# Attention exponentials turned by DMA instead of by TensorE, on eight cores

## The chip, the cores and the metric

The kernel runs on the 8 cores of one Trainium2 chip, each with a program of its own and no traffic between them. The time is the device time in microseconds (us) of the slowest core, the median of several runs. Core 2b+p takes batch row b and half of its query blocks (p is 0 or 1: even or odd blocks of 128), and for these everything that follows.

## What is computed

```
xn = layernorm(x)                                  # x: 4 x 2048 x 2048
q, k, v = split(xn @ w_atten.T)                    # 16 heads of 128
q, k = rope(q), rope(k)
att = softmax(causal(q @ k.T / sqrt(128)))
s = (att @ v) @ w_proj.T
h = silu(xn @ w_gate) * (xn @ w_up)                # 8192 wide
h = the 2 largest of each 4 by magnitude, others 0
out = x + s * silu(h @ w_down)
```

## The kernel before

Each of a core's five engine programs is written out by hand, with semaphores between them. The order is: layernorm of 16 tiles with their transposes and the first 15 units of the projections; the attention stage; 32 groups of the output projection; gate and up with the sparsification; down, and the end.

**Units and steps.** The q, k and v projections are cut into units (`UNITS`): one PSUM bank, 16 steps, a step being a matmul of 512 columns (L443) or two of 256 for v (L432). A group of two heads has 4 units of k and 2 of q for each head, and 8 of v. ScalarE copies a finished unit out of its bank (`leave`, L601 for q and k, L594 for v); for q and k two DMAs of 64 KB then swap the halves of the partitions (from SP, L352 and L353; for the first 15 units from ScalarE, L606 and L607) and VectorE applies rope in three instructions (L726, L728, L738), into one of three buffers of `qh` and `kh`. The weights come in pieces of 512 KB as POOL's DMAs into a ring of six (`ringA`), which the later stages extend to nine (`ringB`).

**Windows.** The attention stage has 128 windows, one for each head and each block of 128 queries; block j of a head has 256(j+1) keys. In window w TensorE computes the scores into PSUM banks 0 to 3 (L520; the mask is added by L522, a matmul with the identity), which needs the exponential of window w-1 to be done, as there is one set of these banks. VectorE takes the maximum (L807) and its negative (L811), ScalarE the exponential in f32 with its sum (L673), VectorE the reciprocal (L795) and the scaled block in bf16 (L801). TensorE fills the window with steps of the projections (`STEPS`, in two parts), and between the parts it transposes the scaled block of window w-1, 128 x 128 at a time, into bank 6 (first eight, L467) and bank 7 (the others, L474). VectorE copies the first eight out (L747), ScalarE the others (L615), into `pT`, which holds two blocks side by side. Every second window TensorE multiplies the values with both blocks (L491, v as weights, 256 columns moving), and ScalarE copies the result, already with d on the partitions, into `y_all` (L620).

Between the windows, SP's queue holds the rope swaps alone. The projection (L539) waits for the last copy to `y_all`.

## Time and profile before

| | us |
|---|---|
| median of 3 runs (2321.11 to 2322.1) | 2322.09 |
| the profiled execution's own time | 2320.11 |
| its span on the slowest core (of 2313.8 to 2318.6) | 2318.6 |
| TensorE busy | 2233.9 (96%) |
| VectorE busy | 996.6 (43%) |
| ScalarE busy | 635.7 (27%) |
| first scores of the attention stage, first projection matmul | 126.0, 903.3 |

The profile takes one execution. A busy time of TensorE counts each matmul from its start to a modelled end, so matmuls overlap; the chain of waits shows the distance between them. A wait is named by what released it. A line such as L467 is a line of the kernel before.

### The profile page before, as it was taken

To read this page: it belongs to the slowest core of one execution; us is meant where nothing else is said; L and a number is where in the kernel's file an instruction comes from. 1 tells how busy PE (TensorE), PEld (TensorE's weight loads), DVE (VectorE), ACT (ScalarE), POOL (GpSimd) and SP (SyncE) were. 2 spreads that over 40 slices of the span, in tenths; PEclk is the share of its full clock that TensorE was granted. 3 is DMA by queue.
4 is the path that set the end of the run, shared out by engine and by line. 5 is a ranking of instruction groups with operands and counts; after the bars stand their busy time and mean duration, and the time that the engine had idled before them with its cause. 6 is when DMAs were issued, how large, how long until landed. Compare 5 with 4: busy or idle time off the path is not lost.

```text
span 2318.6 us, 35747 instructions; the slowest of 8 cores (2313.8 to 2318.6 us)
## 1 busy us (share of the span) xinstructions
PE 2233.9 (96%) x12736; PEld 1181.9 (51%) x12736; DVE 996.6 (43%) x1441; ACT 635.7 (27%) x1082; POOL 137.5 (6%) x260
## 2 busy tenths in 40 slices
PE   4789999999999988999999999999999999999999
PEld 3547566675766744444444444444444444444444
DVE  5566867768677673004444443333333331000111
ACT  4624344444434434122222222222222200000000
POOL 0000000000000000000000000000000000000000
PEclk8999999999999999999999999999999999999999
DMA  9342322223122143754434344444554479766661
GB/s 268 109 79 47 61 40 45 57 44 66 38 46 56 33 79 74 156 111 80 83 74 73 73 80 83 90 94 91 97 101 94 91 168 238 157 127 132 132 138 44
DMA packets 82732, 217.38 MB, mean 94 GB/s; under 512 B 9984, under 2 KB 30592, under 8 KB 80000
## 3 DMA queue, kind: packets, MB, share of 16 engines
q0 software_dynamic: 36864, 134.23, 33.7%
q1 hardware_dynamic: 44576, 79.94, 11.0%
q8 instruction: 107, 1.75, 0.3%
q10 hardware_dynamic: 1120, 0.92, 0.1%
q14 instruction: 65, 0.53, 0.1%
HBM read 311.53 MB, written 25.17 MB: 145 GB/s over the span
## 4 chain that ended last, share of the span: by engine, by line
PE 82%; DVE 7%; issue 5%; DMA 3%; ACT 1%; DVEq 0%; ACTq 0%; SPq 0%
PE ps L554 37%; PE ps L573 19%; PE ps L432 8%; PE ps L443 7%; PE ps L539 5%; DVE arena L807 3%; DMA arena<-arena 2%; PE ps L520 2%; DVE arena L728 2%; PE ps L491 1%; PE ps L467 1%; DMA arena<-xN 1%; DVE arena L726 1%; PE ps L421 1%; DVE arena L738 1%
## 5 line engine op out<-in xcount | busy, mean ns | idle before, releaser
L554 PE MATMUL ps<-arena 128*128 128x512 bf16 x3968 | 856.6, 379 | 0.0
L554 PEld LDWEIGHTS ps<-arena 128*128 128x128 bf16 x3968 | 388.3, 98 | 468.1
L573 PE MATMUL ps<-arena 128*128 128x512 bf16 x2048 | 442.2, 379 | 1.1 <-DVE arena L858 1.1
L443 PE MATMUL ps<-arena 128*128 128x512 bf16 x1536 | 363.1, 385 | 14.2 <-ACT arena L630 14.2
L858 DVE TENSOR_TENSOR arena<-arena,ps 128x512 f32<-128x512 f32 x124 | 85.0, 685 | 633.7 <-PE ps L554 633.7
L573 PEld LDWEIGHTS ps<-arena 128*128 128x128 bf16 x2048 | 200.3, 98 | 242.9 <-issue 1.5
L432 PE MATMUL ps<-arena 128*128 128x256 bf16 x2048 | 241.1, 273 | 1.5 <-ACT arena L630 1.5
L443 PEld LDWEIGHTS ps<-arena 128*128 128x128 bf16 x1536 | 147.0, 99 | 167.6 <-issue 24.7
L696 ACT ACTIVATE arena<-arena 128x512 f32<-128x512 f32 x128 | 80.6, 630 | 519.5 <-DVE arena L858 519.5
L673 ACT ACTIVATE arena<-ps,arena 128x256 f32<-128x256 f32 (+7 forms) x128 | 156.4, 1222 | 230.9 <-DVE arena L811 230.8
L432 PEld LDWEIGHTS ps<-arena 128*128 128x128 bf16 x2048 | 197.1, 98 | 24.9 <-issue 1.8
L807 DVE TENSOR_REDUCE arena<-ps 128x1 f32<-128x256 f32 (+7 forms) x128 | 173.1, 1352 | 27.6 <-PE ps L522 26.7
L868 DVE TENSOR_TENSOR arena<-arena 128x512 f32<-128x512 f32 x32 | 22.2, 692 | 376.3 <-ACT arena L713 372.9
L713 ACT ACTIVATE arena<-ps 128x512 f32<-128x512 f32 x32 | 19.1, 597 | 422.7 <-PE ps L573 422.7
L898 POOL DMA_DIRECT2D arena<-wgu x128 | 67.5, 531 | 868.1 <-PE ps L554 710.8
L801 DVE TENSOR_SCALAR arena<-arena 128x256 bf16<-128x256 f32 (+7 forms) x128 | 104.9, 820 | 26.8 <-DVE arena L795 26.7
L539 PE MATMUL ps<-arena 128*128 128x512 bf16 x512 | 110.7, 379 | 0.6 <-ACT arena L620 0.6
L692 ACT ACTIVATE arena<-ps 128x512 f32<-128x512 f32 x124 | 73.8, 595 | 130.4 <-PE ps L554 130.4
L520 PE MATMUL ps<-arena 128*128 128x512 bf16 (+1 forms) x320 | 83.1, 358 | 18.8 <-ACT arena L673 14.2
L747 DVE COPY arena<-ps 128x1024 bf16<-128x1024 bf16 (+3 forms) x128 | 75.6, 591 | 51.0 <-PE ps L467 47.6
L728 DVE TENSOR_TENSOR arena<-arena 128x512 f32<-128x512 bf16 x96 | 65.9, 686 | 47.7 <-DMA arena<-arena 47.7
L539 PEld LDWEIGHTS ps<-arena 128*128 128x128 bf16 x512 | 50.0, 98 | 60.9 <-issue 0.8
(54 smaller groups left out, 1394.5 us busy)
## 6 DMA issues: line engine op xcount, KB each, us to landing
arena<-wgu POOLq DMA_DIRECT2D x128, 512.0 KB, 6.1
arena<-wd POOLq DMA_DIRECT2D x64, 512.0 KB, 5.8
arena<-wqkv POOLq DMA_DIRECT2D x48, 512.0 KB, 5.7
arena<-xN SPq DMA_DIRECT2D x16, 1024.0 KB, 12.7
arena<-arena SPq DMA_DIRECT2D x178, 64.0 KB, 2.1
arena<-wp POOLq DMA_DIRECT2D x16, 512.0 KB, 6.0
d_s<-arena SPq DMA_DIRECT2D x32, 256.0 KB, 4.0
d_hT<-arena SPq DMA_DIRECT2D x16, 512.0 KB, 6.7
```

Source lines behind the costliest of these rows:

```text
L432: mm = e.matmul(bank[:, (mi // NF) * 256:(mi // NF + 1) * 256], xnv[tc // 8][:, f, (tc % 8) * 128:(tc % 8 + 1) * 128], wv[f // 8][:, f % 8 ...
L443: mm = e.matmul(bank[:], w[:, f, :], xnv[tile // 2][:, f, (tile % 2) * 512:(tile % 2 + 1) * 512], start=(f == 0), stop=(f == NF - 1))
L520: mm = e.matmul(psum[:, c0:c1], qh[h % 3][:, j * 128:(j + 1) * 128], kh[h % 3][:, c0:c1], start=True, stop=(c1 != ncol))
L539: mm = e.matmul(ps[4 + k % 4][:], w[:, yc, :], yav[:, yc, half * 512:(half + 1) * 512], start=(yc == 0), stop=(yc == NF - 1))
L554: mm = e.matmul(ps[2 * p + up][:], w[:, f, :], xnv[0][:, f, half * 512:(half + 1) * 512], start=(f == 0), stop=(f == NF - 1))
L573: mm = e.matmul(ps[2 * (fc % 4) + half][:], w[:, j, :], hT[16 * q + j][:, half * 512:(half + 1) * 512], start=(q == 0 and j == 0), stop=(q ...
L673: e.activation(pexp[:, 0:ncol], psum[:, 0:ncol], AF.Exp, bias=nm[w % 2][:], scale=SCALE, accum_out=den[w % 2][:]).then_inc(S["a_ex"])
L696: e.activation(qv[half][:, r, :], h_sb[m % 2][:], AF.Square).then_inc(S["a_hq"])
L728: e.tensor_tensor(t2[:], xsw[r % 2][:], rsin[:, cols], ALU.mult).then_inc(S["v_t2"])
L801: e.tensor_scalar_mul(pbf[:, 0:ncol], pexp[:, 0:ncol], rc[b][:, 0:1]).then_inc(S["v_nr"])
L807: e.tensor_reduce(mx[b][:], psum[:, 0:ncol], mybir.AxisListType.X, ALU.max).then_inc(S["v_mx"])
L858: e.tensor_tensor(h_sb[m % 2][:], sg[m % 2][:], up[:], ALU.mult).then_inc(S["v_h"])
```

## The change

The exponential is written in bf16, without scaling, into one of two buffers `pexp`. SP turns it by one DMA transpose (`turn_p`, up to 128 x 2048) into one of four buffers `pT`. Three windows later (`LAG`) TensorE multiplies: now each 128 x 128 piece of `pT` is the weights and v moves, 128 columns, so that the result has the queries on the partitions. ScalarE copies it out times the reciprocal of the sum (`leave_y`), into `y_sb`, and SP turns it by a second DMA transpose into `y_all` (`turn_y`). The transposes on TensorE and both copies out of PSUM are gone, and so is VectorE's scaling. The rope swaps are issued from ScalarE throughout. The projections take a third PSUM bank. `STEPS` spreads the same number of steps in another way over the windows. The rings have five and eight buffers in place of six and nine.

```diff
-NRA, NRB = 6, 9
+NRA, NRB = 5, 8
+LAG = 3
...
-STEPS = [17, 18, 19, 20, 20, 21, 22, 23] * (2 * NG - 2)
-STEPS += [12, 13, 13, 14, 14, 14, 12, 12, 12, 12, 12, 13, 13, 13, 14, 15]
-def second_batches(w):
-    return 4 * ((w + 1) // NB) + max(0, (w + 1) % NB - 4)
+STEPS = [14, 15, 16, 21, 22, 23, 24, 25] * (2 * NG - 2)
+STEPS += [8, 9, 11, 16, 17, 19, 18, 18, 7, 8, 10, 12, 13, 13, 14, 15]
...
-    for w in range(NW + 1):
-        pv = (w - 3) // 2 if w % 2 == 1 and w >= 3 else None
-        if w < NW:
-            a = 7 if pv is not None else 9
-            parts = (cut(pos, pos + a), cut(pos + a, pos + STEPS[w]))
-            pos += STEPS[w]
-        else:
-            parts = ([], [])
-        rows.append((pv, parts))
+    for w in range(NW):
+        a = STEPS[w] // 2
+        rows.append((cut(pos, pos + a), cut(pos + a, pos + STEPS[w])))
+        pos += STEPS[w]
     assert pos == 16 * (len(UNITS) - NSTART)
-    return rows
+    return rows + LAG * [([], [])]
...
-    den = [A.alloc(1) for _ in range(2)]
-    rc = [A.alloc(1) for _ in range(2)]
+    den = [A.alloc(1) for _ in range(4)]
+    rc = [A.alloc(1) for _ in range(4)]
+    y_sb = [A.alloc(64, BF16) for _ in range(2)]
...
-    pexp = A.alloc(8 * KB)
-    pbf = A.alloc(4 * KB, BF16)
-    pT = A.alloc(8 * KB, BF16)
-    pTv = pT[:].rearrange("p (k x) -> p k x", x=256)
+    pexp = [A.alloc(4 * KB, BF16) for _ in range(2)]
+    pT = [A.alloc(4 * KB, BF16) for _ in range(4)]
+    pTv = [v[:].rearrange("p (k x) -> p k x", x=128) for v in pT]
...
-        def swap(r):
-            e.wait_ge(S["a_u"], ROPE_UNIT[r] + 1)
-            if r >= 2:
-                e.wait_ge(S["v_t2"], r - 1)
-            e.dma_start(out=xsw[r % 2][0:64, :], in_=raw[r % 2][64:128, :]).then_inc(S[f"dSW{r % 2}"], 16)
-            e.dma_start(out=xsw[r % 2][64:128, :], in_=raw[r % 2][0:64, :]).then_inc(S[f"dSW{r % 2}"], 16)
+        def turn_p(w):
+            e.wait_ge(S["a_ex"], w + 1)
+            if w >= 4:
+                e.wait_ge(S["p_pv"], w - 3)
+            n = 2 * (w % NB + 1)
+            e.dma_start_transpose(out=pTv[w % 4][:, 0:n, :], in_=pexp[w % 2][:, 0:128 * n]).then_inc(S[f"dT{w % 2}"], 16)
+        def turn_y(w):
+            h, j = w // NB, w % NB
+            e.wait_ge(S["a_y"], w + 1)
+            e.dma_start_transpose(out=yav[:, h:h + 1, j * 128:(j + 1) * 128], in_=y_sb[w % 2][:]).then_inc(S[f"dY{w % 2}"], 16)
...
+        for w in range(NW + LAG):
+            if w >= LAG:
+                turn_y(w - LAG)
+            if w < NW:
+                turn_p(w)
...
-                bank = ps[4 + u % 2]
-                if s0 == 0 and u >= 2:
-                    e.wait_ge(S["a_u"], u - 1)
+                bank = ps[4 + u % 3]
+                if s0 == 0 and u >= 3:
+                    e.wait_ge(S["a_u"], u - 2)
...
-        def turn_p(w):
-            n = 2 * (w % NB + 1)
-            e.wait_ge(S["v_nr"], w + 1)
+        def values(w):
+            h, n = w // NB, 2 * (w % NB + 1)
+            e.wait_ge(S[f"dT{w % 2}"], 16 * (w // 2 + 1))
+            e.wait_ge(S["a_u"], max(u for u, un in enumerate(UNITS) if un[:2] == (h // 2, "v")) + 1)
             if w:
-                e.wait_ge(S["v_te"], w)
-            for k in range(min(8, n)):
-                mm = e.transpose(psX[6][:, k, :], pbf[:, k * 128:(k + 1) * 128], id_sb[:])
-            mm.then_inc(S["p_t"])
-            if n > 8:
-                if second_batches(w - 1):
-                    e.wait_ge(S["a_te"], second_batches(w - 1))
-                e.wait_ge(S["a_y"], w // 2 if w % 2 == 0 else (w - 1) // 2)
-                for k in range(8, n):
-                    mm = e.transpose(psX[7][:, k - 8, :], pbf[:, k * 128:(k + 1) * 128], id_sb[:])
-                mm.then_inc(S["p_t1"])
-        def values(pair):
-            h, jj = pair // 4, pair % 4
-            e.wait_ge(S["v_te"], 2 * pair + 2)
-            if second_batches(2 * pair + 1):
-                e.wait_ge(S["a_te"], second_batches(2 * pair + 1))
-            if pair:
-                e.wait_ge(S["a_y"], pair)
-            bank = ps[7]
-            e.wait_ge(S["a_u"], max(u for u, un in enumerate(UNITS) if un[:2] == (h // 2, "v")) + 1)
+                e.wait_ge(S["a_y"], w)
             v = vg[(h // 2) % 2]
-            last = 4 * jj + 3
-            for k in range(last + 1):
-                x0 = 0 if k < 4 * jj + 2 else 128
-                mm = e.matmul(bank[:, x0:256], v[:, k * 256 + (h % 2) * 128:k * 256 + (h % 2 + 1) * 128],
-                              pTv[:, k, x0:256], start=(k == 0), stop=(k == last))
+            for k in range(n):
+                mm = e.matmul(ps[7][:, 0:128], pTv[w % 4][:, k, :],
+                              v[:, k * 256 + (h % 2) * 128:k * 256 + (h % 2 + 1) * 128],
+                              start=(k == 0), stop=(k == n - 1))
             mm.then_inc(S["p_pv"])
...
-            if pv is not None:
-                values(pv)
             steps(parts[0])
-            if w:
-                turn_p(w - 1)
+            if w >= LAG:
+                values(w - LAG)
             steps(parts[1])
-        values(NW // 2 - 1)
         for k in range(32):
...
-                e.wait_ge(S["a_y"], NW // 2)
+                e.wait_ge(S["a_u"], len(UNITS))
+                e.wait_ge(S["dY0"], 16 * (NW // 2))
+                e.wait_ge(S["dY1"], 16 * (NW // 2))
...
-                e.copy(raw[r % 2][:], ps[4 + u % 2][:]).then_inc(S["a_u"])
-                if u < NSTART:
-                    e.wait_ge(S["a_u"], u + 1)
-                    if r >= 2:
-                        e.wait_ge(S["v_t2"], r - 1)
-                    e.dma_start(out=xsw[r % 2][0:64, :], in_=raw[r % 2][64:128, :]).then_inc(S[f"dSW{r % 2}"], 16)
-                    e.dma_start(out=xsw[r % 2][64:128, :], in_=raw[r % 2][0:64, :]).then_inc(S[f"dSW{r % 2}"], 16)
-        def leave_p(w):
-            e.wait_ge(S["p_t1"], second_batches(w))
-            if w // 2:
-                e.wait_ge(S["p_pv"], w // 2)
-            n = 2 * (w % NB + 1) - 8
-            e.copy(pTv[:, 8:8 + n, (w % 2) * 128:(w % 2 + 1) * 128], psX[7][:, 0:n, :]).then_inc(S["a_te"])
-        def leave_y(pair):
-            h, jj = pair // 4, pair % 4
-            e.wait_ge(S["p_pv"], pair + 1)
-            e.copy(yav[:, h, jj * 256:(jj + 1) * 256],
-                   ps[7][:, 0:256]).then_inc(S["a_y"])
+                e.copy(raw[r % 2][:], ps[4 + u % 3][:]).then_inc(S["a_u"])
+                e.wait_ge(S["a_u"], u + 1)
+                if r >= 2:
+                    e.wait_ge(S["v_t2"], r - 1)
+                e.dma_start(out=xsw[r % 2][0:64, :], in_=raw[r % 2][64:128, :]).then_inc(S[f"dSW{r % 2}"], 16)
+                e.dma_start(out=xsw[r % 2][64:128, :], in_=raw[r % 2][0:64, :]).then_inc(S[f"dSW{r % 2}"], 16)
+        def leave_y(w):
+            e.wait_ge(S["p_pv"], w + 1)
+            e.wait_ge(S["v_rc"], w + 1)
+            if w >= 2:
+                e.wait_ge(S[f"dY{w % 2}"], 16 * (w // 2))
+            e.activation(y_sb[w % 2][:], ps[7][:, 0:128], AF.Copy, scale=rc[w % 4][:, 0:1]).then_inc(S["a_y"])
...
+        for w, parts in enumerate(WINDOWS):
             if w < NW:
                 ncol = 256 * (w % NB + 1)
                 e.wait_ge(S["v_nm"], w + 1)
-                if w:
-                    e.wait_ge(S["v_nr"], w)
                 if w >= 2:
-                    e.wait_ge(S["v_rc"], w - 1)
-                e.activation(pexp[:, 0:ncol], psum[:, 0:ncol], AF.Exp, bias=nm[w % 2][:], scale=SCALE,
-                             accum_out=den[w % 2][:]).then_inc(S["a_ex"])
-            if w and (w - 1) % NB >= 4:
-                leave_p(w - 1)
-            for u in LEAVE_LATE[w]:
+                    e.wait_ge(S[f"dT{w % 2}"], 16 * (w // 2))
+                if w >= 4:
+                    e.wait_ge(S["v_rc"], w - 3)
+                e.activation(pexp[w % 2][:, 0:ncol], psum[:, 0:ncol], AF.Exp, bias=nm[w % 2][:], scale=SCALE,
+                             accum_out=den[w % 4][:]).then_inc(S["a_ex"])
+            for u in ended(parts[0]):
                 leave(u)
-        leave_y(NW // 2 - 1)
+            if w >= LAG:
+                leave_y(w - LAG)
+            for u in ended(parts[1]):
+                leave(u)
...
-        def leave_p(w):
-            e.wait_ge(S["p_t"], w + 1)
-            if w // 2:
-                e.wait_ge(S["p_pv"], w // 2)
-            n = min(8, 2 * (w % NB + 1))
...
-        for w, (pv, parts) in enumerate(WINDOWS):
-            if w:
-                b, ncol = (w - 1) % 2, 256 * ((w - 1) % NB + 1)
-                e.wait_ge(S["a_ex"], w)
-                if w >= 3:
-                    e.wait_ge(S["v_nr"], w - 2)
-                e.reciprocal(rc[b][:], den[b][:]).then_inc(S["v_rc"])
-                e.wait_ge(S["v_rc"], w)
-                if w >= 2:
-                    e.wait_ge(S["p_t"], w - 1)
-                    if (w - 2) % NB >= 4:
-                        e.wait_ge(S["p_t1"], second_batches(w - 2))
-                e.tensor_scalar_mul(pbf[:, 0:ncol], pexp[:, 0:ncol], rc[b][:, 0:1]).then_inc(S["v_nr"])
+        for w in range(NW + 1):
...
-                    wait_piece_free(e, NA - NRA + b)
+                    wait_piece_free(e, NA - NRA + (b - NA) % NRA)
```

**TensorE, windows 7 and 8 of a head.** Before (L520 and L522 scores and mask, L443 and L432 steps, L467 and L474 transposes, L491 values of two blocks):

```order
L520 MATMUL ps<-arena 128x512 x3
L520 MATMUL ps<-arena 128x256
L522 MATMUL ps<-arena 128x256
L443 MATMUL ps<-arena 128x512 x9
L467 MATMUL ps<-arena 128x128 x8
L474 MATMUL ps<-arena 128x128 x4
L443 MATMUL ps<-arena 128x512 x13
L520 MATMUL ps<-arena 128x512 x4
L522 MATMUL ps<-arena 128x256
L491 MATMUL ps<-arena 128x256 x10
L491 MATMUL ps<-arena 128x128 x2
```

After (L496 and L498 scores and mask, L429 steps, L466 values of one block):

```order
L496 MATMUL ps<-arena 128x512 x3
L496 MATMUL ps<-arena 128x256
L498 MATMUL ps<-arena 128x256
L429 MATMUL ps<-arena 128x256 x24
L466 MATMUL ps<-arena 128x128 x8
L429 MATMUL ps<-arena 128x256 x24
```

The 12 transposes between the steps are gone; in their place stand the 8 value matmuls of the block three windows before, and the window has 24 steps (48 matmuls of 256 columns), where it had 22 (of 512 there).

**ScalarE, from the exponential of a head's seventh block to the eighth's or past it.** Before (L673 exponential, L615 copy of transposes, L601 exit of a q or k unit, L620 exit of y):

```order
L673 ACTIVATE arena<-ps,arena 128x1792
L615 COPY arena<-ps 128x4x128
L601 CAST arena<-ps 128x512
L620 CAST arena<-ps 128x256
L601 CAST arena<-ps 128x512
L673 ACTIVATE arena<-ps,arena 128x2048
L615 COPY arena<-ps 128x6x128
L601 CAST arena<-ps 128x512
L673 ACTIVATE arena<-ps,arena 128x256
```

After (L637 exponential, L576 exit of a unit, L580 and L581 its swap, L589 exit of y with the scaling):

```order
L637 ACTIVATE arena<-ps,arena 128x1792
L576 CAST arena<-ps 128x512
L580 DMA arena<-arena 64x512
L581 DMA arena<-arena 64x512
L589 ACTIVATE arena<-ps,arena 128x128
L576 CAST arena<-ps 128x512
L580 DMA arena<-arena 64x512
L581 DMA arena<-arena 64x512
L637 ACTIVATE arena<-ps,arena 128x2048
L576 CAST arena<-ps 128x512
L580 DMA arena<-arena 64x512
L581 DMA arena<-arena 64x512
```

The copy of transposes is gone, and behind every exit of a q or k unit stand two DMA issues ahead of the next instruction.

**SP, the attention stage.** Before (L352, L353 swaps), with the waits:

```order
L353 DMA arena<-arena 64x512
L352 DMA arena<-arena 64x512 [waits a_u,v_t2]
L353 DMA arena<-arena 64x512
L352 DMA arena<-arena 64x512 [waits a_u,v_t2]
L353 DMA arena<-arena 64x512
L352 DMA arena<-arena 64x512 [waits a_u,v_t2]
```

After (L343 the exponentials' transposes, L349 y's):

```order
L343 DMA_TRANSPOSE arena<-arena 128x16x128 [waits a_ex,p_pv]
L349 DMA_TRANSPOSE arena<-arena 128x1x128 [waits a_y]
L343 DMA_TRANSPOSE arena<-arena 128x2x128 [waits a_ex,p_pv]
L349 DMA_TRANSPOSE arena<-arena 128x1x128 [waits a_y]
L343 DMA_TRANSPOSE arena<-arena 128x4x128 [waits a_ex,p_pv]
L349 DMA_TRANSPOSE arena<-arena 128x1x128 [waits a_y]
```

The swaps have left the queue; a transpose of y that waits for ScalarE's exit stands ahead of each transpose of exponentials.

## Rows read from the trace of the kernel before

**Rows 1.** The table of stretches (busy time and instructions of each engine, granted clock, DMA share, GB/s)

```profile
126.00:898.00 772.00, 744.89 (x5568) 486.30 (x5568) 553.72 (x910) 312.62 (x535) 28.38 (x51) 1.00 0.27 52
260.00:700.00 440.00, 431.81 (x3315) 291.03 (x3314) 318.97 (x524) 179.08 (x306) 13.72 (x26) 1.00 0.25 48
800.00:898.00 98.00, 85.72 (x611) 49.97 (x609) 67.18 (x109) 42.56 (x71) 7.27 (x11) 1.00 0.35 63
```

**Rows 2.** TensorE's waits, 126 to 915 us (total, times, longest)

```profile
PE ps L520 <- ACT arena L673: 14.2, 23, 2.2
PE ps L467 <- DVE arena L801: 11.0, 17, 2.1
```

**Rows 3.** The chain of waits, 500 to 530 us (start, us, what)

```profile
507.36 0.45 PE ps L467 x8
...
508.03 2.84 PE ps L432 x26
...
515.35 3.45 PE ps L443 x16
...
523.91 1.64 PE ps L491 x16
```

**Rows 4.** Groups by form, whole span (busy, mean ns, idle before)

```profile
L491 PE MATMUL ps<-arena 128*128 128x256 bf16 x512 | 67.7, 276 | 2.6 <-ACT arena L615 2.6
...
L467 PE MATMUL ps<-arena 128*128 128x128 bf16 x832 | 67.2, 219 | 11.7 <-DVE arena L801 11.0 <-issue 0.5
...
L474 PE MATMUL ps<-arena 128*128 128x128 bf16 x320 | 28.3, 219 | 0.0
...
L491 PE MATMUL ps<-arena 128*128 128x128 bf16 x128 | 17.6, 219 | 0.0
```

**Rows 5.** The page, costliest groups: VectorE's scaling and copies

```profile
L801 DVE TENSOR_SCALAR arena<-arena 128x256 bf16<-128x256 f32 (+7 forms) x128 | 104.9, 820 | 26.8 <-DVE arena L795 26.7
...
L747 DVE COPY arena<-ps 128x1024 bf16<-128x1024 bf16 (+3 forms) x128 | 75.6, 591 | 51.0 <-PE ps L467 47.6
```

**Rows 6.** TensorE's waits, 800 to 898 us

```profile
PE ps L467 <- DVE arena L801: 2.1, 1, 2.1
```

**Rows 7.** The chain of waits, 885 to 915 us

```profile
890.01 2.30 DVE arena L807
...
894.69 0.20 ACT arena L673
...
899.57 3.13 PE ps L491 x16
...
903.30 11.81 PE ps L539 x54
```

**Rows 8.** Groups by form, VectorE's maximum and ScalarE's exponential of a first block

```profile
L673 ACT ACTIVATE arena<-ps,arena 128x256 f32<-128x256 f32 x16 | 7.6, 474 | 27.7 <-DVE arena L811 27.7
...
L807 DVE TENSOR_REDUCE arena<-ps 128x1 f32<-128x256 f32 x16 | 6.7, 421 | 0.6
```

**Rows 9.** The page, DMA issues (count, KB each, us to landing)

```profile
arena<-wqkv POOLq DMA_DIRECT2D x48, 512.0 KB, 5.7
...
arena<-arena SPq DMA_DIRECT2D x178, 64.0 KB, 2.1
...
d_hT<-arena SPq DMA_DIRECT2D x16, 512.0 KB, 6.7
```

**Rows 10.** Instructions in order of time, TensorE, 126 to 136 us

```profile
126.03 0.37 PE L520 MATMUL ps<-arena 128*128 128x256 bf16 x1 [4.55 <-DVE arena L738]
...
126.41 6.05 PE L443 MATMUL ps<-arena 128*128 128x512 bf16 x17
```

**Rows 11.** Instructions in order of time, ScalarE, 95 to 126 us

```profile
122.40 0.47 ACTq L606 DMA_DIRECT2D arena<-arena  x1
122.90 0.71 ACTq L607 DMA_DIRECT2D arena<-arena  x1
```

**Rows 12.** VectorE's waits, 126 to 915 us

```profile
DVE arena L728 <- DMA arena<-arena: 31.2, 23, 4.5
```

35 lines of the change are left out of this document (14 added, 21 removed).

## The prediction

> **What bounds the kernel now.** I read the table of stretches first, then TensorE's waits, the chain of waits, and last the single forms and the DMA issues. The stretch that the change touches is the attention stage, from the first scores at 126 us [rows 10] to the first projection matmul at 903.3 [rows 7], so 777 us. The table shows TensorE busy for 744.9 us of its first 772, at a granted clock of 1.00 (2.4 GHz), VectorE for 554 and ScalarE for 313; in the 440 us from 260 to 700 TensorE idles 8.2 us in all [rows 1]. TensorE's waits of the whole stage are short: 14.2 us on the exponential before the next scores, 11.0 on the scaled block before its transposes [rows 2]. So TensorE's own work is the bound, and a matmul taken away there comes off the time, as long as what replaces it keeps up.
>
> The chain of waits gives the spacing of back to back matmuls, which the busy times (219 or 272 ns each) hide: 8 transposes in 0.45 us, so 0.056 us each; 26 matmuls of 256 columns in 2.84, so 0.109; 16 of 512 columns in 3.45, so 0.2155; 16 of the values in 1.64, which is 14 x 0.109 + 2 x 0.056 [rows 3]. The last one matters: a value matmul of 128 columns, with its own weight load, also costs 0.056.
>
> **The change part by part.** Where no sign of time is given, it is TensorE's path in the attention stage.
>
> 1. The transposes go. There are 832 + 320 of them [rows 4]; 1152 x 0.056 = **-64.5 us**.
>
> 2. The values are turned round and done per block of 128 queries. Before: 512 x 0.109 + 128 x 0.056 = 63.0 us [rows 3, 4]. After: 72 matmuls per head of 128 columns, 1152 x 0.056 = 64.5. **+1.5 us**.
>
> 3. VectorE loses the scaling of the exponentials (104.9 us) and the copies out of PSUM (75.6) [rows 5], ScalarE the second copies. That is no time by itself, but TensorE's waits for the scaling go with it; of their 11.0 us, 2.1 lie between 800 and 898 us [rows 6] and are counted next, the other 8.9 here: **-9 us**. Between 800 and 898 us TensorE idles 12.3 us [rows 1], because the last windows hold few projection steps and the chain scores, maximum, exponential is longer than TensorE's work. That chain stays, without the scaling in VectorE's way. For the last block of a head it is 0.97 of scores and mask, 0.15 to start, and from 890.01 to 894.89 maximum and exponential [rows 7]: 6.1 us; for the first 2.0 (maximum 0.42, exponential 0.47 [rows 8]), and the six between them spaced evenly. Against it stands TensorE's work by the new step counts. In the last head, 15 steps x 0.2155 + 0.97 + 10 values x 0.056 = 4.8 for the last block; over its eight windows the chain exceeds the work by 4.6 us, over those of the head before by 1.0. So 12.3 becomes 5.6: **-7 us**. In all other heads the work of a window (3.9 us with 14 steps, 6.9 with 25) is above its chain (2.0 to 6.1), so nothing is added there.
>
> 4. The tail. Before, from the end of the last exponential at 894.89 to the projection at 903.30 it is 8.4 us: scaling, 16 transposes, copies, 16 value matmuls in 3.13 us (half the clock), copy [rows 7]. Now: issue 0.5, landing of 512 KB, 16 values at the low clock 1.8, their exit 0.4, issue 0.5, landing of y 2.1, 0.2 of semaphores. The landing of a 512 KB transpose is in no row; plain transfers of that size took 5.7 and 6.7 us, 64 KB within SBUF 2.1 [rows 9]; I take 6.2. Sum 11.7, so +3.3. Steps 1 and 2 counted 1.6 us of this stretch as saved, which goes back on. The projection starts cold: after the 4.55 us pause that ended at 126 us, 17 matmuls took 6.05 in place of 3.66 [rows 10], +2.4. Together **+7 us**.
>
> 5. The transposes of all other blocks are hidden if two limits hold. Latency: an exponential waits for the transpose of two blocks before, since there are two buffers. It is tightest behind the last block of a head, followed by the two shortest windows: 0.8 us left of its own window, 3.9 of the next and 1.6 of the second until ScalarE wants the buffer, so 6.3, and 1.8 more (4.3 of work less 2.5 of chain) until TensorE waits for the scores' bank. The values come three windows later, 14 us or more. A landing of 6.2 just fits. Throughput: a head needs 72 + 8 blocks of 32 KB in 43.3 us of TensorE's work (160 steps, 3.9 us of scores, 0.9 of masks, 4.0 of values), so up to 0.54 us a block costs nothing. Rows give 5.7 to 6.7 us for 16 blocks' bytes, 0.36 to 0.42 a block, at their whole latency; at the other end the swaps of rope, 64 KB in 2.1, give 1.05 [rows 9]. I take the nearer in size, the 512 KB ones: **0 us**, and keep 1.05 for a rival.
>
> The Trainium skill, VectorE: DVE Perf Modes, The three transpose paths, speaks against this: it gives 1309 ns for a 128 x 128 transpose by DMA against 390 on TensorE. One after the other, the DMA ones would make 80 x 1.309 = 105 us a head and, as an estimate, 3220 us for the kernel. Its 390 ns is a lone instruction: the trace has 56 ns in a row [rows 3], so the 1309 is likely to be latency as well. The Trainium skill's DMA: Bandwidth & Descriptors, Latency and other measured facts, has 261 GB/s for DMA transposes, by which 512 KB move in 2.0 us; an estimate by that page leaves the sum as it is. No run here shows either.
>
> 6. The swaps of rope move from SP's queue to ScalarE's. SP's queue is then the transposes' alone: it issues the y of three blocks before, then the block's own; y waits for the middle of the window, which is before the exponential's end for the long blocks and 1 us after it for the shortest. On ScalarE two issues take 0.47 and 0.71 [rows 11], so 82 units put 97 us on an engine that is busy for 313 of 772 [rows 1], and each issue stands ahead of an exponential or an exit. A window has 0.8 to 1.9 us of slack against its chain. Where two rope units end in one window (2 x 1.9 us with their exits, exponential 2.2, y 0.4) ScalarE is just inside 6.9. VectorE waited 31 us for swaps in this stage already [rows 12], and transposes now share the rings. Between nothing and 0.4 us for each of 82 (33 us) I take **+6 us**, near the low end, as VectorE has 180 us less to do.
>
> 7. The ring of five and eight, one bank more for the projections: POOL waits long for free pieces today, a piece lands in 5.7 us [rows 9], and eight units (some 36 us) lie between the release that decides and the use. 0. If the ring were late, TensorE would wait at a first step of a unit; I see no place.
>
> Sum: -64.5 + 1.5 - 9 - 7 + 7 + 6 = **-66 us** on the profiled execution's 2320.1 us (span 2318.6 and 1.5 around it), so 2254. The median of the runs is 2.0 above that execution: **2256 us**.
>
> **Rivals.** A measurement of this kernel can tell about 0.2% (4.6 us) from no change.
>
> A. As summed, 56%. Its own range is 2244 (no cost in step 6, and a landing of 4 us) to 2280 (step 6 at 0.4 us each).
>
> B. Faster, but a wait takes back about half. ScalarE's queue, with swap issues that also wait for rope's second product two units before, delays exponentials, and swaps land behind 512 KB transposes, so that VectorE holds the next maximum. At 0.4 us for each unit plus the DVE wait of 31 us doubled and half exposed: 2256 + 27 + 15 = 2298. For it: one swap in four already makes VectorE wait. Against: a swap has most of a window. 16%.
>
> C. The other side. The transposes are slower than TensorE: SP's single queue turns one block at a time, and the bound is 80 blocks a head. At the swap's 1.05 us a block a head takes 84 us, the stage 1344, the kernel 2322 + 567 = 2889. It binds from 0.54 us a block, and loses from 48.6 / 80 = 0.61; at 0.67 it is 2400. For it: small rows within SBUF are the only such transfers the trace has, and their rate is low. Against: large ones run at 0.4. 24%, a third of it below 2400; 5 of the 24 for blocks that go one at a time at over 1.05 us each, towards the 2.1 us of a whole swap, which would be over 2889. The Trainium skill's 1309 ns (The three transpose paths) would lie there, at 3220 by the estimate above.
>
> D. No change. If each value matmul waited for its weight load, they would be spaced 0.109 instead of 0.056: 1152 x 0.053 = +61 us, 2317 or, with the rest of step 6, 2322. The 16 value matmuls in 1.64 us [rows 3] speak against it. 4%.
>
> **The numbers.** Faster by over 0.2%: A and B, 0.72. Same: D, 0.04. Slower: C, 0.24. Range 2244 to 2400: below it 2% of A, above it about 16% of C.
>
> **What would show it.** Right: no transposes on TensorE in the attention stage, 1152 value matmuls in 0.056 us each by the chain, stage of 711 us at the full clock, transposes of 512 KB landing in under 8 us, ScalarE's exponential waiting for the maximum and not for a DMA, a pause of 10 us before the projection. Step 5 is wrong if the exponentials wait for DMA or SP's queue is never idle; step 6 if TensorE's scores wait for an exponential that came behind a swap. A stage over 777 us makes the prediction wrong in sign.

## The result: slower by 1.4%, where 2.8% faster was forecast

The change takes 2352.10 us (2351.69 to 2361.73), the kernel before 2322.1 (2321.11 to 2323.11). The ratio is 1.0142, with a 95% interval of 1.0112 to 1.0173. In some executions of either kernel the cores of one or both dies show a lower clock and the time is some per cent longer; these are left out of every time and ratio here (with the one of 2679.2 us the median of the change is 2356.91, the 2357 of the expectations below). The forecast was 2256 us: the time lies in its range of 2244 to 2400, on the wrong side. In the profile of the change cores 0 and 1 show a granted clock of 0.81 for some 115 us; the stage is therefore compared on core 5 below, which has none of it and whose span is nearly as long.

The spans of the changed kernel by core, with the mean granted clock (before: 2313.8 to 2318.6, 0.992 to 0.994):

```profile
core 1: 2360.0 us, clock 0.965
...
core 4: 2331.8 us, clock 0.979
core 5: 2357.5 us, clock 0.978
```

The whole attention stage in the table of stretches, core 5. First the kernel before:

```profile
126.00:903.30 777.30, 748.07 (x5585) 488.44 (x5586) 554.19 (x910) 314.13 (x538) 28.38 (x51) 0.99 0.27 52
```

the change:

```profile
123.00:940.70 817.70, 711.80 (x4944) 446.01 (x4945) 393.37 (x655) 284.29 (x539) 26.92 (x51) 0.94 0.62 101
```

This is where the time is. The stage was to shrink from 777 to 711 us and grew to 817.7. TensorE has its matmuls taken away (busy 748 to 712), yet idles 105.9 us where it idled 29.2. The granted clock falls from 0.99 to 0.94: it was at half (1.2 GHz) for 92 us of this stage on core 5, for 67 to 92 on the eight cores, before for 8 to 17. VectorE has lost 161 us of its work (554.19 to 393.37). The DMA engines' share went from 0.27 to 0.62.

What ended the waits in the stage, core 1 (engine, line, releaser; total, times, longest). The scores are L496 now, the exponential L637, the value matmuls L466, rope's product with the swap L693:

```profile
DVE arena L693 <- DMA arena<-arena: 103.7, 33, 8.3
PEld ps L496 <- issue: 99.7, 63, 8.0
PE ps L496 <- ACT arena L637: 79.7, 29, 7.6
...
ACT arena L637 <- DMA arena<-arena: 53.4, 10, 10.6
...
PE ps L466 <- DMA arena<-arena: 4.6, 1, 4.6
```

Against [rows 2]: TensorE's wait for the exponential before the next scores rose from 14.2 us to 79.7. The waits for the scaling are gone, and TensorE hardly waits for the turned block itself. The late ones are one step earlier: ScalarE waits for a DMA, 10 times and up to 10.6 us, which is the transpose (here called a turn) of two windows before, and VectorE waits for rope's swaps (31.2 us in [rows 12]).

The page of the change, groups and DMA issues (the value matmuls, then the issues with us to landing last):

```profile
L466 PE MATMUL ps<-arena 128*128 128x128 bf16 x1152 | 93.2, 231 | 8.7 <-DMA arena<-arena 4.6
...
arena<-wqkv POOLq DMA_DIRECT2D x48, 512.0 KB, 6.5
arena<-arena ACTq DMA_DIRECT2D x192, 64.0 KB, 2.8
```

The pieces landed in 5.7 us before, the swaps in 2.1 [rows 9].

**One such wait from the start.** Core 1, 482 to 500 us, in order of time (start, us; in brackets the idle time before and its releaser). The exponential of a head's seventh block ends at 479.37, and y's exit (L589) of three blocks before stands on ScalarE behind an exit and two swap issues:

```profile
479.18 0.19 ACT L637 ACTIVATION_READ_ACCUMULATOR arena<-ps,arena 128x1 f32 x1
...
481.30 0.37 ACT L589 ACTIVATE arena<-ps,arena 128x128 bf16<-128x128 f32 x1 [1.45 <-issue]
```

SP's queue, where L349 is the turn of y and L343 that of a block (the one at 482.99 the seventh block's, the one at 489.67 the eighth's):

```profile
481.74 1.10 SPq L349 DMA_TRANSPOSE arena<-arena  x1
482.99 1.44 SPq L343 DMA_TRANSPOSE arena<-arena  x1
488.42 1.11 SPq L349 DMA_TRANSPOSE arena<-arena  x1
489.67 8.02 SPq L343 DMA_TRANSPOSE arena<-arena  x1
```

POOL's queue, which loads the weight pieces:

```profile
483.34 0.53 POOL L833 DMA_DIRECT2D arena<-wqkv  x1 [17.53 <-PE ps L440]
```

ScalarE, with the swaps that it issues:

```profile
486.52 0.47 ACTq L580 DMA_DIRECT2D arena<-arena  x1
487.02 0.74 ACTq L581 DMA_DIRECT2D arena<-arena  x1
...
497.65 0.47 ACT L637 ACTIVATE arena<-ps,arena 128x256 bf16<-128x256 f32 x1 [8.84 <-DMA arena<-arena]
```

VectorE, then TensorE:

```profile
489.04 0.69 DVE L691 TENSOR_TENSOR arena<-arena 128x512 f32<-128x512 bf16 x1
497.90 0.69 DVE L693 TENSOR_TENSOR arena<-arena 128x512 f32<-128x512 bf16 x1 [8.17 <-DMA arena<-arena]
```

```profile
489.15 1.67 PE L440 MATMUL ps<-arena 128*128 128x512 bf16 x7
498.36 0.59 PE L496 MATMUL ps<-arena 128*128 128x512 bf16 x1 [7.54 <-ACT arena L637]
```

The chain of waits over the same stretch has the transfer itself as one piece:

```profile
482.99 14.52 DMA arena<-arena
```

The turn of the seventh block (1792 columns, 448 KB) leaves at 482.99, 3.6 us after its exponential, as y's turn stands ahead of it and waits for the exit. A 512 KB weight piece follows 0.35 us later. The turn lands at 497.51, after 14.5 us, where I had 6.2 for a larger one. SP's next turn of a block takes 8 us to issue. The two swaps issued at 486.52 and 487.02, 64 KB each, land at 497.42 and 497.81, so two things are late at once: ScalarE may not write the buffer that is being turned, and VectorE stands in rope with the next maximum behind it. TensorE has used up its steps and stops for 7.5 us, and then goes on at half the clock:

```profile
484.00:489.00 5.00, 5.00 (x33) 2.49 (x31) 4.42 (x9) 3.23 (x5) 0.00 (x0) 1.00 1.17 103
498.40:501.00 2.60, 2.60 (x10) 1.41 (x11) 2.22 (x5) 0.08 (x1) 0.45 (x1) 0.50 0.53 118
```

From the trace's DMA records, over all cores, and counting a weight piece as in flight when over 20 of its packets move during the turn: the turn of a head's seventh block (448 KB) lands in 4.0 us (median) without one and in 9.1 with one (longest 4.8 and 15.4), that of the eighth in 5.9 and 8.8. Of 128 turns a core, 26 to 30 take over the 6.3 us that step 5 allowed; 212 of these 226 have a piece in flight. A turn also leaves late: on the eight cores 1.6 to 3.6 us after the end of its exponential (medians by block of a head; 3.2 for the seventh, 2.6 for the eighth), behind y's.

### The profile page after: what moved, and what is told of

Its sections match the earlier page's. It is cut to its first block, busy times and chain, and to the rows that moved or that the text cites. A ratio compares the mean times of both kernels' runs of the same rounds, so it can differ in the third digit from the quotient of the medians.

```text
span 2360.0 us, 34216 instructions; the slowest of 8 cores (2331.8 to 2360.0 us)
## 1 busy us (share of the span) xinstructions
PE 2218.7 (94%) x12096; PEld 1148.6 (49%) x12096; DVE 835.4 (35%) x1185; ACT 604.6 (26%) x1082; POOL 135.8 (6%) x260
## 4 chain that ended last, share of the span: by engine, by line
PE 81%; DMA 10%; DVE 3%; issue 3%; ACT 2%; ACTq 1%; SPq 0%; DVEq 0%
PE ps L529 36%; PE ps L548 19%; PE ps L429 9%; DMA arena<-arena 9%; PE ps L440 7%; PE ps L514 5%; PE ps L496 2%; PE ps L466 2%; DVE arena L752 1%; DMA arena<-xN 1%; DVE arena L693 1%; ACT arena L576 1%; ACTq L580 1%; DVE arena L722 0%; ACT arena L637 0%
## 5 line engine op out<-in xcount | busy, mean ns | idle before, releaser
L529 PE MATMUL ps<-arena 128*128 128x512 bf16 x3968 | 856.6, 379 | 0.0
L529 PEld LDWEIGHTS ps<-arena 128*128 128x128 bf16 x3968 | 388.3, 98 | 468.2
L548 PE MATMUL ps<-arena 128*128 128x512 bf16 x2048 | 442.2, 379 | 1.1 <-DVE arena L808 1.1
L440 PE MATMUL ps<-arena 128*128 128x512 bf16 x1536 | 385.5, 400 | 13.1 <-ACT arena L598 13.1
L548 PEld LDWEIGHTS ps<-arena 128*128 128x128 bf16 x2048 | 200.3, 98 | 242.9 <-issue 1.5
L637 ACT ACTIVATE arena<-ps,arena 128x256 bf16<-128x256 f32 (+7 forms) x128 | 156.3, 1221 | 432.7 <-DVE arena L762 347.4
L429 PE MATMUL ps<-arena 128*128 128x256 bf16 x2048 | 252.5, 281 | 1.0 <-ACT arena L598 1.0
L440 PEld LDWEIGHTS ps<-arena 128*128 128x128 bf16 x1536 | 153.3, 102 | 181.1 <-issue 63.3
L429 PEld LDWEIGHTS ps<-arena 128*128 128x128 bf16 x2048 | 204.5, 101 | 34.2 <-issue 4.2
L496 PE MATMUL ps<-arena 128*128 128x512 bf16 (+1 forms) x320 | 87.7, 374 | 82.0 <-ACT arena L637 79.7
L514 PE MATMUL ps<-arena 128*128 128x512 bf16 x512 | 112.9, 384 | 3.0 <-DMA arena<-arena 3.0
L693 DVE TENSOR_TENSOR arena<-arena 128x512 f32<-128x512 bf16 x96 | 66.0, 687 | 120.5 <-DMA arena<-arena 120.5
L466 PE MATMUL ps<-arena 128*128 128x128 bf16 x1152 | 93.2, 231 | 8.7 <-DMA arena<-arena 4.6
L466 PEld LDWEIGHTS ps<-arena 128*128 128x128 bf16 x1152 | 82.3, 105 | 34.8 <-issue 19.2
L496 PEld LDWEIGHTS ps<-arena 128*128 128x128 bf16 x320 | 30.2, 99 | 121.3 <-issue 102.5
## 6 DMA issues: line engine op xcount, KB each, us to landing
arena<-xN SPq DMA_DIRECT2D x16, 1024.0 KB, 10.8
```

The source lines that it names most:

```text
L429: mm = e.matmul(bank[:, (mi // NF) * 256:(mi // NF + 1) * 256], xnv[tc // 8][:, f, (tc % 8) * 128:(tc % 8 + 1) * 128], wv[f // 8][:, f % 8 ...
L440: mm = e.matmul(bank[:], w[:, f, :], xnv[tile // 2][:, f, (tile % 2) * 512:(tile % 2 + 1) * 512], start=(f == 0), stop=(f == NF - 1))
L466: mm = e.matmul(ps[7][:, 0:128], pTv[w % 4][:, k, :], v[:, k * 256 + (h % 2) * 128:k * 256 + (h % 2 + 1) * 128], start=(k == 0), stop=(k = ...
L496: mm = e.matmul(psum[:, c0:c1], qh[h % 3][:, j * 128:(j + 1) * 128], kh[h % 3][:, c0:c1], start=True, stop=(c1 != ncol))
L514: mm = e.matmul(ps[4 + k % 4][:], w[:, yc, :], yav[:, yc, half * 512:(half + 1) * 512], start=(yc == 0), stop=(yc == NF - 1))
L529: mm = e.matmul(ps[2 * p + up][:], w[:, f, :], xnv[0][:, f, half * 512:(half + 1) * 512], start=(f == 0), stop=(f == NF - 1))
```

## The experiments

All ratios are against the kernel before, run on the same chip between them (2323.3 us for the first four, 2325.6 for e5 to e8, 2324.9 for e9 to e12, 2324.4 for the last two), and compare means, so that a time quoted below, a median, can differ from them a little. The table below gives, from each trace, the range over the eight cores. "Maxima late" is how much later than the usual 0.12 us after the end of the scores the maximum began, summed over 128 blocks; "exponentials late" is the same from the negative maximum to the exponential. Not all of either stops TensorE, as the first row shows: the kernel before has its maxima later still, but in short pieces. TensorE waited over 2 us before a block's scores 2 or 3 times in its stage, 15 to 19 times in the change's and once or twice in e13's.

| kernel | ratio, 95% | stage, us | TensorE idle | half clock | maxima late | exponentials late |
|---|---|---|---|---|---|---|
| before | | 775–779 | 26–36 | 8–17 | 115–126 | 17–18 |
| the change | 1.0142 (1.0112 to 1.0173) | 788–818 | 87–106 | 67–92 | 93–107 | 45–76 |
| e1 small swaps | 1.0014 (0.9983 to 1.0045) | 766–782 | 74–86 | 37–64 | 86–99 | 41–55 |
| e2 small pieces | 0.9844 (0.9760 to 0.9928) | 729–753 | 44–53 | 21–33 | 54–59 | 40–48 |
| e3 both | 0.9838 (0.9786 to 0.9891) | 721–733 | 37–51 | 14–33 | 49–53 | 41–50 |
| e4 plain copies | 0.9963 (0.9929 to 0.9997) | 753–774 | 65–77 | 22–60 | 99–112 | 26–33 |
| e5 three buffers | 1.0154 (1.0087 to 1.0221) | 776–809 | 73–98 | 62–91 | 107–130 | 27–37 |
| e6 late rope | two runs: 0.997, 1.002 | 763–773 | 67–89 | 46–63 | 13–17 | 106–126 |
| e7 quarters | 1.0042 (1.0018 to 1.0067) | 765–774 | 71–87 | 36–58 | 73–88 | 65–76 |
| e8 all three | 0.9833 (0.9817 to 0.9850) | 723–733 | 39–52 | 27–38 | 14–21 | 47–57 |
| e9 whole start | 0.9776 (0.9731 to 0.9822) | 716–740 | 35–55 | 23–45 | 11–22 | 48–62 |
| e10 late, quarters | 1.0027 (1.0016 to 1.0037) | 749–779 | 59–84 | 34–52 | 13–16 | 109–142 |
| e11 late, three | 0.9855 (0.9806 to 0.9903) | 726–743 | 42–55 | 28–43 | 17–27 | 50–66 |
| e12 before, swaps moved | 1.0017 (1.0005 to 1.0029) | 776–788 | 30–43 | 6–14 | 110–123 | 27–32 |
| e13 last burst spread | 0.9716 (0.9692 to 0.9739) | 708–721 | 27–43 | 18–25 | 11–20 | 42–49 |
| e14 three, quarters | 0.9893 (0.9862 to 0.9925) | 732–749 | 44–59 | 22–43 | 74–86 | 27–32 |

**Less to move: e1 to e4.** These four move other data than the kernel needs, and so compute something else. The change with swaps of 16 columns in place of 512 after the first 15 units:

```diff
+                m = 512 if u < NSTART else 16
-  ...xsw[r % 2][0:64, :], in_=raw[r % 2][64:128, :]...
+  ...xsw[r % 2][0:64, 0:m], in_=raw[r % 2][64:128, 0:m]...
```

> The change, with the rope swaps of the attention windows cut to 16 of 512 columns (same DMAs, waits and order; q and k are wrong). Theory S (the swaps land late behind the transposes, and VectorE, which runs its work in order, holds the next maximum for them): VectorE's waits for DMA in the windows (74 us between 260 and 800 us) fall only if the bytes matter; if the swap's packets stand behind those of a transpose, a small swap lands as late and the time stays at 2352 to 2360. Theory P (ScalarE's issues of the swaps are what costs): unchanged, 2357. Theory B (it is the bytes of the swaps): about 45 us of TensorE's waits go, and half of the cold clock behind them, 2300.

2325.05 us, 1.3% under the change: between theory B's 2300 and the unchanged time of the others. But VectorE's wait for the swaps hardly moved in the profile, from 120.5 us over the span to

```profile
DVE arena L694 <- DMA arena<-arena: 109.3, 36, 9.3
```

though a swap carries 1/32 of the bytes. So a swap is late mostly through what is ahead of it or beside it, not through its own size; what fell a little are the long turns (20 to 25 of 128 over 6.3 us) and the half clock. The weight pieces cut to 64 of 2048 columns from the seventh on:

```diff
+                m = 2048 if n < 6 else 64
-                e.dma_start(out=ringA[p % NRA][:], in_=wqkv[p])...
+                e.dma_start(out=ringA[p % NRA][:, 0:m], in_=wqkv[p][:, 0:m])...
```

> The change, with the weight pieces of the attention stage from the seventh on cut to 64 of 2048 columns (same DMAs, waits and order; the projections are wrong). Theory C (collision: a transpose and a weight piece in flight together slow each other, turns of the seventh block land in 7 to 15 us in place of 4.4): the turns land in 4 to 6 us, ScalarE's exponential no longer waits for DMA, about 30 us of TensorE's waits and the cold clock behind them go: 2300 to 2315. Rival T (the transposes alone are slow enough, since two buffers allow 6.3 us): under 10 us of gain, 2350.

2300.18 us (2276 to 2303), 2.9% under the change, as theory C said: the turns land as they do alone (block 8 at 5.4 to 6.1 us, 5 to 8 of 128 over 6.3), and the maxima's lateness shrinks by over 40%. But the exponentials still wait for turns, 7 to 12 of them a core. Both cuts together:

> Both cuts together. If bytes of other DMAs beside the transposes are all that is wrong, the forecast's 2256 comes back (within 15 us). If the transposes alone delay each other and the small DMAs behind them, it stays above 2290, with VectorE still waiting for swaps that land after a 512 KB transpose.

2291.43 us, two of six executions at 2270: once the pieces are gone, the swaps' bytes are worth nothing that the intervals tell. Nor does the forecast come back: TensorE still idles 37 to 51 us, and the exponentials are as late as in e2. Last, each transpose as a plain copy of the same bytes, so that nothing is turned:

```diff
-            e.dma_start_transpose(out=pTv[w % 4][:, 0:n, :], in_=pexp[w % 2][:, 0:128 * n])...
+            e.dma_start(out=pT[w % 4][:, 0:128 * n], in_=pexp[w % 2][:, 0:128 * n])...
```

> The change, with both transposing DMAs replaced by plain copies of the same bytes within SBUF (the values are wrong). Theory X (it is the transpose's form, packets of 256 B, 2048 of them for 512 KB, that fills the DMA engines): with rows of up to 4 KB the copies take a fraction, 64 KB swaps do not wait, about 2256 to 2270. Theory Y (it is the traffic within SBUF as such, or the two buffers): copies land in 4 us or more for 512 KB and the time stays at 2320 or above.

2315.8 us, near theory Y and far from X. The transposing form costs 1.8%; block 8 lands in 4.7 to 5.4 us in place of 6.7 to 8.3 (medians by core). But the maxima are as late as in the change (99 to 112 us): what holds the swaps up is not the form of the transfers beside them. What did fall is the exponentials' lateness (26–33 us for 45–76), and besides the shorter landing SP takes 0.5 us to issue a copy and 1.4 a turn, so that a block's leaves 1.0 to 3.0 us after its exponential, not 1.6 to 3.6.

**The right result with the waits mended: e5 to e8.** Smaller, packed places for the exponentials, so that one waits for the turn of three windows before:

```diff
-                if w >= 2:
-                    e.wait_ge(S[f"dT{w % 2}"], 16 * (w // 2))
+                if w >= 3:
+                    e.wait_ge(S[f"dT{(w - 3) % 4}"], 16 * ((w - 3) // 4 + 1))
```

> The change with three buffers for the exponentials in place of two (in the same space: each block's buffer has the block's own size). An exponential then waits for the transpose of three blocks before. Theory L (about a third of TensorE's waits, 24 to 48 us a core, come from exponentials that wait for a late transpose): these go, with some of the cold clock behind them; 2357 becomes 2315 to 2330. Rival (late swaps and a slow maximum carry it all): under 10 us.

2352.8 us (2349.71 to 2381.18), 1.0154 by the means: nothing gained, as the rival said. The exponentials' lateness did fall, from 45–76 to 27–37 us, and the maxima's rose, from 93–107 to 107–130. Next, rope one window later on VectorE, with a third pair of buffers for it, and to make room its two products in bf16 (the lines for both are left out here):

```diff
-                for u in LEAVE[w - 1]:
+                for u in LEAVE[w - 2] if w > 1 else []:
```

> The change with rope's three instructions one window later on VectorE, and three buffers for what they read (their two products in bf16 to make room). Theory S (45 us a core of TensorE's waits stand behind a maximum that VectorE holds for a swap landing late): 2357 becomes 2300 to 2320. Rival (ScalarE's queue holds the exponentials, the swaps' landing does not matter): unchanged.

Two executions, 2317.74 and 2329.69 us, 1.2 to 1.7% under the change and level with before. Here the exchange goes the other way: the maxima are on time (13–17 us), and the exponentials' lateness doubled (106–126). The products in bf16 may have a part in this, as each of rope's three instructions fell from 0.69 to 0.42 us; no run moves rope without them. In its trace TensorE still waits 62.9 us for the exponential (79.7 in the change), with ScalarE's wait for the turns behind it:

```profile
ACT arena L637 <- DMA arena<-arena: 123.6, 23, 13.1
...
PE ps L496 <- ACT arena L637: 62.9, 30, 11.0
...
DVE arena L693 <- DMA arena<-arena: 44.5, 12, 9.9
```

Third, each weight piece in quarters, each quarter held back until a given window:

```diff
+                at = PACE[n % 6]
+                for i in range(4):
+                    w = 16 * (n // 6 - (2 if n % 6 == 0 else 1)) + at[i]
...
+                    e.dma_start(out=ringA[p % NRA][:, 512 * i:512 * i + 512], in_=...)
```

> The change with each weight piece of the attention stage loaded as four DMAs of 128 KB, each released in the middle of a window, instead of 512 KB when a ring buffer comes free. Theory C (a whole piece in flight, 5.7 to 12 us, delays turns and swaps): most of what the small pieces brought, so 2300 to 2325. If it is the amount of bytes and not their bunching: 2345 to 2357.

2334.65 us, 1.0% under the change, between the two figures. Its first pieces go in quarters as well, and the stage begins at 133 to 139 us, 11 later than in the change; the stage itself is some 30 us shorter. And all three:

> The three together. If TensorE's work bounds again, the forecast's 2256, at most 2275, and under the kernel before by 2 to 3%. If the DMA engines stay the bound, above 2290.

2286.45 us (2285 to 2288), again between the two figures: 1.7% under before and 3.0% under the change, where the three alone gave 0, some 1.5 and 1.0. They are not a sum, as the pairs below show.

**Which of them, and the swaps' move by itself: e9 to e12.** The first six pieces whole again:

> All three edits together (exponentials in packed buffers of three windows, rope one window later, weight pieces in quarters at fixed places of TensorE's order), but the first six pieces go whole again. In the run of all three the attention stage began at 133 to 136 us in place of 121 to 128, because the first pieces went in quarters. Theory: that delay is a plain addition, so the stage starts at 121 to 128 again and keeps its 723 to 733 us; the kernel takes 2275 to 2280. Rival: what is started earlier is waited for later (the projections of the first windows are ahead of their data), then 2284 to 2288, with a longer stage.

2269.18 us (2266 to 2282), 0.6% less than e8 by the ratios: the stage begins at 120 to 125 us, no wait takes that back. The pairs:

> Rope one window later and weight pieces in quarters, without the packed buffers. Alone, they brought the maximum's lateness away (about 1.5%) and shortened the turns' tail (1.0%). Theory 1, separate causes that add: 2357 less 35 less 20, 2300 or a little above; then the packed buffers give the last 15 of all three together although they gave nothing alone, because only with short tails is the third window of grace enough. Theory 2, one cause seen twice (late landings of any kind): 2312 to 2320, and the packed buffers are the larger part of what all three gave.

2331.52 us, above both theories' figures: without the third buffer, the quarters add nothing to the late rope (its stage is some 4 us shorter than e6's on the mean of the cores and begins 10 us later).

> Rope one window later and packed buffers of three windows, weight pieces whole as in the change. With rope out of VectorE's way, what is left are exponentials that wait for a turn of two windows before (106 to 126 us of them late); a third window of grace should take away every wait for a turn of less than about 10 us. Theory: 2290 to 2300, stage of 735 to 745 us on every core. Rival: whole pieces still draw the turns out to 13 to 20 us, so TensorE waits at the values in place of the scores (over 20 us of idle there): 2310 to 2320.

2287.67 us (2284 to 2301), stages of 726 to 743: the theory's figures or a little under. But the rival's sign is there as well: TensorE waits 21 to 37 us a core at the values. Alone, one edit is worth nothing and the other 1.2 to 1.7%; the pair takes 2.8% off. Then the kernel before, with only the swaps moved to ScalarE's queue:

```diff
-                if u < NSTART:
-                    e.wait_ge(S["a_u"], u + 1)
+                e.wait_ge(S["a_u"], u + 1)
...
-                    swap(ROPE_NO[u])
```

> The kernel before, with all swaps of rope issued from ScalarE's queue, as the change does, and nothing else. Step 6 of the prediction took +6 us for that, between 0 and +33. Theory of the long landings: the swaps are late in the change because they land behind 512 KB turns, not because of the queue that issues them; here no turns exist, so the kernel takes 2322 to 2332, VectorE waits for swaps no more than its 31 to 48 us, and TensorE's stage keeps 777 to 787 us. Rival: the two issues in front of exponentials and exits are themselves the cost: 2345 or more.

2328.09 us, +4 us by the ratio (+1 to +7). VectorE waits hardly longer for its swaps (47.7 us over the span before), and they land nearly as fast:

```profile
DVE arena L715 <- DMA arena<-arena: 49.3, 27, 8.5
```

```profile
arena<-arena ACTq DMA_DIRECT2D x192, 64.0 KB, 2.4
```

**The last two.** In e9, with all other pieces in quarters, the turns over 11 us were, but for one or two at blocks 120 and 121 behind them, the same two on every core: block 117 (11.3 to 12.3 us) and block 119 (15.6 to 30.1), and just there whole pieces leave together, on core 7 three at 774 us and three at 788, and one more at 796.5. The chain of e9 on core 7 has the longest, and TensorE's row shows its price:

```profile
790.17 30.12 DMA arena<-arena
```

```profile
820.64 1.86 PE L473 MATMUL ps<-arena 128*128 128x128 bf16 x16 [22.48 <-DMA arena<-arena]
```

e13 spreads the second burst:

```diff
+                    e.wait_ge(S["p_s"], NW - 7 + [0, 1, 3][b - NRA])
```

> The version with all three edits and a whole start, and besides the three weight pieces of the projection, which leave together when the last rope is done (787 us), go out one by one with the first, second and fourth block of the last head. In the profile of that version the turn of block 119, issued just then, landed after 16 to 30 us on the eight cores, and TensorE idled 18 to 38 us at the values, most of it there. Theory (a turn is drawn out by whole weight pieces in flight on the same DMA engines): the turn of block 119 lands in under 12 us, the idle time at the values falls to 5 to 15 us, and the kernel takes 2255 to 2265. Rival (the long landing belongs to the place: the writes of the head before, or the ends of rope): it stays over 15 us and the kernel at 2270 to 2276.

2260.39 us. The turn of block 119 lands in 10.2 to 16.1 us, under the theory's 12 on four cores and over it on the others, where it was 15.6 to 30.1; the idle time at the values fell to 11 to 21 us (the theory said 5 to 15). The first burst was left, and block 117 still takes 11 to 12 us.

> Packed buffers of three windows and weight pieces in quarters after a whole start, rope where the change has it. Theory (two waits stand one behind the other, the maximum held up by a late swap and the exponential held up by a late turn, and mending one alone leaves the other): rope still holds the maximum, so the packed buffers still give nothing, and this takes what the quarters alone gave less the shorter start, 2320 to 2330, with the maxima late by over 70 us a core. Rival (it was the long tail of the turns alone that made rope late): 2290 or less.

2296.36 us (2294 to 2315): nearer the rival. With rope where the change has it, the packed buffers, worth nothing beside whole pieces (e5), come with a shorter stage once the pieces go in quarters: 732 to 749 us against 765 to 774 in e7, some 29 us or 1.2%. A few of these can be the whole start, by which the stage was 4 us shorter on the mean from e8 to e9. Its maxima are still late by 74 to 86 us, as the theory said, against 107 to 130 in e5. So my account of two waits in series was too strict: with quarters both kinds of lateness are smaller.

**e13 beats both kernels**: 2.8% under before (2.6 to 3.1), 4.2% under the change. Its stage on core 5:

```profile
121.20:839.50 718.30, 680.80 (x4944) 435.58 (x4945) 321.92 (x655) 285.28 (x539) 92.31 (x175) 0.98 0.79 115
```

## Why the prediction was wrong, step by step

The step that failed is 5, "a landing of 6.2 just fits ... 0 us": a turn beside a weight piece took 9 us (median) and up to 15, and it left SP's queue 1.6 to 3.6 us after its exponential. With it failed the half of step 6 that looked at the swaps' issues and not at their landing. TensorE idled 87 to 106 us in the stage, where it had idled 26 to 36.

**Steps 1 and 2 were right.** The 1152 value matmuls run at 0.056 us each, as the chain of the change shows before the last window:

```profile
920.74 0.45 PE ps L466 x8
```

Between before and e13 TensorE's busy time in the stage fell by 748.07 - 680.80 = 67.3 us, for a forecast of 63.0. Rival D is out.

**Step 3 was right in one half.** The waits for the scaling are gone. But of the last two heads it said that 5.6 us of idle time stay, 4.6 of them in the last. From the last scores of the head before to those of the last, TensorE idles 13 to 18 us in the change, 15 to 18 in e2 and 10 to 17 in e13, where the kernel before had 3 to 4. Some 7 of them lie before the scores of the last head's first block, in the change, e2 and e4 alike; in e13 it is 2. The -7 was no gain.

**Step 4 was right.** The chain of the change at the end of the stage:

```profile
930.48 1.10 SPq L349
...
931.72 5.59 DMA arena<-arena
...
937.66 1.88 PE ps L466 x16
...
940.17 2.20 DMA arena<-arena
...
942.51 7.54 PE ps L514 x24
```

From the end of the exponential (930.14) to the projection it is 12.4 us (11.7 in the sum); y's turn ahead takes 1.1 of them, which the sum did not have, the landing is 5.6 (6.2), and the first 24 matmuls take 7.54 - 24 x 0.2155 = 2.4 us more than at the full clock, exactly the +2.4. But this turn has few other transfers beside it, and that was one error of step 5: a duration taken from such rows was used as the worst case.

**Step 5, throughput: right.** Rival C did not happen. From the DMA records the turns' packets fill the 16 engines for 30 to 32% of the stage. The last turn's whole landing is 0.35 us for a block of 128 by 128 (5.6 us for 16), under the limit of 0.54; its packets lie within 2.9 us of that, at some 200 KB per us and up to 280. The Trainium skill has 261 GB/s for DMA transposes (DMA: Bandwidth & Descriptors, Latency and other measured facts), and these records agree in size. The Trainium skill's 1309 ns for one 128 x 128 transpose (VectorE: DVE Perf Modes, The three transpose paths) does not describe blocks in one large DMA, by the 0.35 us measured.

**Step 5, latency: wrong, in two terms.** The limits were worked out as 6.3 us for ScalarE and 1.8 more for TensorE, counted from the end of the exponential. The first term is the landing: 26 to 30 turns a core took over 6.3 us, up to 15, 212 of 226 with a weight piece in flight. "A piece lands in 5.7 us" stood in step 7 and the turn in step 5, and nowhere the two together, though some 42 pieces at 6.5 us are in flight for a third of the stage. e2 and e13 show that link.

The second term was put at nothing: the turn's place in SP's queue. Step 6 had y ready "before the exponential's end for the long blocks"; its exit ended 0.3 to 2.3 us after it (medians by block, 0.75 for the two longest), and y's own issue takes 1.1 more. The eighth block's turn so left 2.6 us late, and with a landing of 5.9 us even alone that is 8.5, not 6.3. On the eight cores 97 exponentials began over 0.2 us late for their turn. In 56 of them the lateness is less than the time that the turn had stood in the queue, so that, as an estimate, they would not have waited had it left at once; in e2, with the landings short, in 59 of 70. That fits what e2 and e3 left over (exponentials late by 40 to 50 us), but no run issues a block's turn ahead of y's, so its cost in time is not shown.

**Step 6.** The issues from ScalarE cost 4 us in e12 (1 to 7), for +6. In the change they also stand ahead of y's exit and so of the next turn, which e12, without turns, cannot show. The swaps' landing behind a turn was the unpriced part. In the change VectorE waited 120.5 us for them over the span, 47.7 before, and the maximum stands behind rope in its program. The 161 us that VectorE was relieved of in the stage did not help, since it waits for a DMA and not for its own work.

**Step 7 was right.** Among TensorE's waits in the change none is for a weight piece. One slip in the range: by its own terms rival A goes from 2248 to 2283, not from 2244 to 2280.

**Rival B** had the mechanism in words ("swaps land behind 512 KB transposes, so that VectorE holds the next maximum") at 2298 us and 16%. It doubled VectorE's wait of 31 us (it came to 103.7 on core 1) and counted half as exposed. It left out that the exponentials wait for turns as well, and the half clock after a pause, 67 to 92 us a core.

**The account on core 5**, change against e13: the stage is 99.4 us longer, 68.4 of it idle time of TensorE (105.9 against 37.5), 31.0 the same 4944 matmuls being busy for longer (711.80 against 680.80) with 92 us of half clock against 23. With the waits mended the kernel takes 2260, the stages are 708 to 721 us, and the forecast had 2256 and 711. That they meet so closely is partly luck: e13 has third buffers, paced pieces and products in bf16 that the forecast had not, and in its last head TensorE idles 10 to 17 us for step 3's 4.6.

**What stays open.** What of the transposing form's 1.8% is its landing and what its longer issue was not taken apart, nor what turning a block ahead of y would give, nor what rope's products in bf16 gave. Where in the DMA engines a swap or a turn is held up (in their order of packets or at the memories) no run shows. A version with both bursts spread was not tried.

## What to carry to other kernels

When a transfer within the chip's memory takes a place in a chain that had none, price it with the large loads in flight, not from rows where it runs alone, and set its longest landing, not its median, against the slack in windows. Count from when its queue lets it go: what stands ahead of it there, and what that waits for, comes first. Look then for small transfers that an engine waits for in program order: they become late behind the large ones, shrinking them helped little here (1.3%), and with their consumer one window on the maxima were on time. Two such waits can hide each other, so a mend that gives nothing alone (the third buffer) may be worth over 1% beside the next one; try them in pairs.

## What the runs showed of the hardware that I had not expected

- A transpose DMA of 448 KB and a weight load of 512 KB issued within 0.4 us of each other landed after 14.5 and 11.6 us; such a transpose without a load took 4.0 (median), such a load in the kernel before 5.7. Two swaps of 64 KB issued 3.5 and 4.0 us behind that transpose landed after 10.9 and 10.8 us, for 2.8 in the median. In e9 a transpose of 512 KB beside three such loads, and a fourth later, took 30.1.
- SP took 1.1 us to issue a transpose DMA of 32 KB and 1.4 (median) for a block's (ScalarE 0.5 to 0.7 for a swap), and 8.0 for the one issued while that of 448 KB was moving: its queue was blocked for that long, to 0.2 us after the landing.
- Swaps of 16 columns were waited for nearly as long as those of 512, 109.3 against 120.5 us in all (core 1).
- After a pause of TensorE of 7.5 us the granted clock was 0.50 for about 5 us (to 503.3; work began again at 498.4). On core 5 the change had 69 us more of such clock in its stage than e13, and the same matmuls were busy for 31 us longer.
